# A fused state-space and channel-mix block on one core: transposed t and the gate's sums in one PSUM bank, values in another, powers interleaved, last unit in halves

## What is computed

```python
xn = layernorm(x)
A_t = sigmoid(A_param)[:, None] ** arange(L)
conv = causal_conv(xn, C_vec * A_t * B_vec) + D_vec * xn      # per channel, along the sequence
z = gelu(conv) @ W_proj.T + b_proj
y = layernorm(xn + z) * gamma + beta
t = x + layernorm(y)
ts = layernorm(t); prev = ts shifted by one row in its sequence, first row 0
r = sigmoid((mu_r * ts + (1 - mu_r) * prev) @ W_r.T)
k = square(relu((mu_k * ts + (1 - mu_k) * prev) @ W_k.T))
out = t + layernorm(r * (k @ W_v.T))
```

## Time and profile before

| | |
|---|---|
| runs | 156.83, 157.89, 156.50 us; median 156.83 |
| profiled execution | 156.51 us, of which its span (first to last instruction) 154.7 us |
| granted TensorE clock, mean | 0.986 |
| PE busy | 137.6 us (89% of the span), 955 matmuls |
| PE weight load busy | 118.0 us (76%) |
| DVE busy | 131.8 us (85%), 371 instructions |
| ACT busy | 130.9 us (85%), 391 instructions |
| POOL busy | 129.0 us (83%), 196 instructions |
| moved | 4.59 MB read, 4.19 MB written, 57 GB/s over the span |
| chain that ended last | PE 74%, DVE 9%, POOL 7%, ACT 4%, issue 2%, DMA 2% |

### The profile page before, as it was taken

How to read it: one execution, slowest core, us unless ns; L and a number is a source line. 1 busy time by engine, 2 the same in 40 slices (tenths; PEclk the granted TensorE clock), 3 DMA queues, 4 the chain that set the end, 5 groups by cost and what they waited for, 6 DMA issues and landing times.

```text
span 154.7 us, 3289 instructions
## 1 busy us (share of the span) xinstructions
PE 137.6 (89%) x955; PEld 118.0 (76%) x955; DVE 131.8 (85%) x371; ACT 130.9 (85%) x391; POOL 129.0 (83%) x196
## 2 busy tenths in 40 slices
PE   3968968887999999999999999999999999999700
PEld 3957857874979797997979977997797798777600
DVE  0999899999899899999999799899989968351783
ACT  5719999699988959988997999979988979999900
POOL 4478997998979886989999899988998989998650
PEclk9999999999999999999999999999999999999995
DMA  3789910000000000100200020020200000414444
GB/s 91 205 226 311 326 35 2 0 0 0 6 0 0 0 4 0 43 29 4 68 0 0 0 70 5 0 70 6 68 0 0 0 4 2 136 59 145 136 126 144
DMA packets 18688, 8.98 MB, mean 58 GB/s; under 512 B 1520, under 2 KB 18672, under 8 KB 18672
## 3 DMA queue, kind: packets, MB, share of 16 engines
q1 hardware_dynamic: 18384, 8.79, 19.5%
q10 hardware_dynamic: 288, 0.00, 0.1%
HBM read 4.59 MB, written 4.19 MB: 57 GB/s over the span
## 4 chain that ended last, share of the span: by engine, by line
PE 74%; DVE 9%; POOL 7%; ACT 4%; issue 2%; DMA 2%; SPq 0%; POOLq 0%; DVEq 0%
PE ps_r L669 9%; PE ps_tv L677 9%; PE ps_r L668 9%; PE ps_k L657 9%; PE ps_k L658 9%; PE ps_z L635 7%; PE ps_prefix L618 7%; PE ps_tv L648 4%; PE ps_prefix L620 3%; PE ps_z L636 3%; PE ps_xT L611 3%; POOL xn_pow L206 3%; DMA x_all<-in_x 2%; POOL x_r L193 2%; DVE x_raw L403 1%
## 5 line engine op out<-in xcount | busy, mean ns | idle before, releaser
L299 ACT ACTIVATE xn<-x_all,x_bias,x_r 128x128 f32<-128x128 f32 x64 | 26.4, 492 | 1.1 <-POOL x_bias L195 1.1
L669 PE MATMUL ps_r<-mixed_T,tsT 128*128 128x128 f32 x128 | 24.7, 275 | 0.0
L668 PE MATMUL ps_r<-mixed_T,tsT 128*128 128x128 f32 x128 | 24.7, 275 | 0.0
L356 ACT ACTIVATE f_normal<-f,out_bias,f_r 128x128 f32<-128x128 f32 x56 | 23.0, 488 | 0.4 <-POOL out_bias L249 0.4
L635 PE MATMUL ps_z<-pv_T,gelu 128*128 128x128 f32 x128 | 22.4, 277 | 0.7 <-ACT gelu L313 0.6
L206 POOL TENSOR_TENSOR xn_pow<-xn,pow_token 128x512 f32<-128x512 f32 x16 | 20.4, 1278 | 2.6 <-DVE pow_token L539 2.1
L635 PEld LDWEIGHTS ps_z<-pv_T,gelu 128*128 128x128 f32 x128 | 19.4, 191 | 1.8 <-issue 0.9
L668 PEld LDWEIGHTS ps_r<-mixed_T,tsT 128*128 128x128 f32 x128 | 19.6, 192 | 1.0 <-issue 1.0
L618 PE MATMUL ps_prefix<-prefix_ones,xn_pow 128*128 128x256 f32 x64 | 19.3, 384 | 1.0 <-POOL xn_pow L206 1.0
L669 PEld LDWEIGHTS ps_r<-mixed_T,tsT 128*128 128x128 f32 x128 | 19.4, 192 | 0.0
L319 ACT ACTIVATE junk<-ps_z 128x128 f32<-128x128 f32 x64 | 16.7, 277 | 3.1 <-PE ps_z L636 3.1
(11 more groups left out here) (86 smaller groups left out, 362.6 us busy)
## 6 DMA issues: line engine op xcount, KB each, us to landing
out_x<-x_all SPq DMA_DIRECT2D x16, 256.0 KB, 2.2
x_all<-in_x SPq DMA_DIRECT2D x7, 512.0 KB, 5.9
x_all<-in_x SPq DMA_DIRECT2D x2, 128.0 KB, 3.1
x_all<-in_x SPq DMA_DIRECT2D x1, 256.0 KB, 3.5
...
```

The lines of the kernel that those rows point to most:

```text
L299: last = a_.activation(tile(xn[u % D], j), xa(u, j), ACT.Identity, bias=col(x_bias, u, j), scale=col(x_r, u, j))
L356: last = a_.activation(tile(f_normal[u % D], j), tile(f[u % D], j), ACT.Identity, bias=col(out_bias, u, j), scale=col(f_r, u, j))
L668: t_.matmul(tile(ps_r, j), tsT[u % D][:, q, l + 1:l + 1 + P], mixed_T[:, 0, :], start=True, stop=False)
L669: last = t_.matmul(tile(ps_r, j), tsT[u % D][:, q, l:l + P], mixed_T[:, 1, :], start=False, stop=True)
```

## The change

It does the following.

- **PSUM.** Transposed t and the gate's sums share the bank ps_tr; the values have ps_v. `transpose_t(u)` now waits for `tanh_r(u - 1)` instead of `gate(u - 2)`, and `values(u)` no longer waits for a copy of transposed t. `gates(u)` waits for `copy_tT(u)` as before, which now also frees its bank.
- **Powers.** Each step waits for the one before by its own count, and unit 0's statistics and variances are placed between the steps. DVE no longer waits for the constants before them.
- **Start on PE.** 18 fillers at the start instead of 28, 18 instead of 14 after unit 0, and 10 more before transpose_xn(4); unit 0's transposes and prefix sum come before the transposes of W_proj and W_v.
- **Scales.** y's and f's statistics share one tensor, so that one product in `f_scale_of` makes both means; the product y_mean_r in `y_scale_of` is gone.
- **Last unit.** Unit 15's gate, statistics, scales, last add and store are done in two halves of two tiles.
- **T_ON_POOL** gains unit 1.
- **All four lists** are in a new order.

The diff, cut to its core (names that only follow the new tensors are left out):

```diff
-T_ON_POOL = (3, 5, 7, 9, 11, 13)
+T_ON_POOL = (1, 3, 5, 7, 9, 11, 13)
...
-        ps_xT, ps_prefix, ps_z0, ps_z1, ps_z2, ps_tv, ps_k, ps_r = (
+        ps_xT, ps_prefix, ps_z0, ps_z1, ps_z2, ps_tr, ps_k, ps_v = (
...
+            for h in range(2):
+                sp.wait_ge(out_half, h + 1)
+                sp.dma_start(out_dram[:, LAST * TILES + 2 * h:LAST * TILES + 2 * h + 2, :],
+                             xa(LAST, 2 * h, 2).rearrange("p (n c) -> p n c", c=P)).then_inc(stored, 16)
...
             def f_scale_of(u, n):
...
-                g_.tensor_tensor(cols(f_mean_r, u, n), cols(f_raw, u, n)[:, :, 1], cols(f_r, u, n),
+                g_.tensor_tensor(yf_mean_r[:, u:u + n, :, :], yf_raw[:, u:u + n, :, :, 1], yf_r[:, u:u + n, :, :],
                                  ALU.mult).then_inc(f_mean_done, n)
...
+            def f_scale_half(h):
+                j = 2 * h
+                pool.wait_ge(f_half_stats, h + 1)
+                g_.tensor_scalar(f_ve[:, LAST, j:j + 2], yf_raw[:, LAST, 1, j:j + 2, 2], 1.0 / P, 4 * EPS, ALU.mult,
+                                 ALU.add).then_inc(half_chain, 1)
...
...
-            def x_first_half(h):
+            def x_first_half_stats(h):
                 dve.wait_ge(x_first[h], 16)
-                link(pair_stats(x_raw, 2 * h, xa(0, 2 * h, 2)))
+                pair_stats(x_raw, 2 * h, xa(0, 2 * h, 2)).then_inc(x_first_stats, 1)
+            def x_first_half_variance(h):
+                dve.wait_ge(x_first_stats, h + 1)
...
+            def gate_half(h):
+                a, b = 2 * h * P, (2 * h + 2) * P
+                dve.wait_ge(tanh_done, UNITS)
+                dve.wait_ge(v_ready, UNITS)
+                after(dve, f_scaled, LAST - D + 1)
+                v_.scalar_tensor_tensor(f[LAST % D][:, a:b], tanh[LAST % D][:, a:b], 1.0, ps_v[:, a:b], ALU.add,
+                                        ALU.mult).then_inc(f_half, 1)
...
...
+            def power_step(k):
+                n = 1 << k
+                dve.wait_ge(s_powers, k + 1)
+                v_.tensor_scalar(pow_up[:, n + 1:2 * n + 1], pow_up[:, 1:n + 1], pow_up[:, n:n + 1], None,
+                                 ALU.mult).then_inc(s_powers, 1)
...
-            x_first_half(0)
-            x_first_half(1)
-            powers(0, 8).then_inc(s_powers, 1)
-            x_pooled(1, 1)
+            power_step(0)
+            x_first_half_stats(0)
+            power_step(1)
+            x_first_half_variance(0)
+            power_step(2)
+            x_first_half_stats(1)
+            power_step(3)
+            x_first_half_variance(1)
+            power_step(4)
+            power_step(5)
+            power_step(6)
+            power_step(7)
+            link(x_stats(1))
+            x_variance(1, 1).then_inc(x_moments, 1)
...
             def transpose_t(u):
...
-                after(pe, f_ready, u - 1)
+                after(pe, tanh_done, u)
...
             def values(u):
-                pe.wait_ge(tT_copied, min(u + 2, UNITS))
                 pe.wait_ge(k_act_ready, u + 1)
```

More of the change, by code:

```diff
@@ L348, in tanh_r @@
                 after(act, f_ready, u - D + 1)
-                a_.activation(tanh[u % D][:], ps_r[:], ACT.Tanh, scale=0.5).then_inc(tanh_done, 1)
+                a_.activation(tanh[u % D][:], ps_tr[:], ACT.Tanh, scale=0.5).then_inc(tanh_done, 1)
             def scale_f(u):
@@ L676, in values @@
                 for j in range(TILES):
-                    last = t_.matmul(tile(ps_tv, j), tile(k_act[u % D], j), pv_T[:, 1, :], start=True, stop=True)
+                    last = t_.matmul(tile(ps_v, j), tile(k_act[u % D], j), pv_T[:, 1, :], start=True, stop=True)
                 last.then_inc(v_ready, 1)
             centre_bias()
-            transpose_pv(); transpose_xn(0); prefix_sum(0); keep_busy(14); transpose_xn(1); prefix_sum(1)
-            project(0); prefix_sum(2); transpose_xn(2); project(1); transpose_xn(3); prefix_sum(3); project(2)
@@ L683, in _ @@
-            transpose_rk(); transpose_xn(4); prefix_sum(4); project(3); mix_weights(); prefix_sum(5)
-            transpose_xn(5); project(4); transpose_t(0); keys(0); gates(0); transpose_xn(6); transpose_t(1)
-            prefix_sum(6); project(5); values(0); keys(1); transpose_xn(7); gates(1); transpose_t(2); project(6)
-            prefix_sum(7); keys(2); values(1); prefix_sum(8); transpose_xn(8); transpose_t(3); project(7); gates(2)
-            keys(3); transpose_xn(9); prefix_sum(9); values(2); gates(3); project(8); transpose_xn(10)
@@ L688, in _ @@
-            transpose_t(4); prefix_sum(10); values(3); keys(4); project(9); gates(4); transpose_t(5); prefix_sum(11)
-            transpose_xn(11); project(10); values(4); keys(5); gates(5); transpose_t(6); prefix_sum(12)
-            transpose_xn(12); values(5); project(11); gates(6); keys(6); transpose_t(7); transpose_xn(13)
-            prefix_sum(13); project(12); keys(7); values(6); transpose_xn(14); prefix_sum(14); gates(7)
-            prefix_sum(15); transpose_t(8); project(13); values(7); keys(8); transpose_t(9); transpose_xn(15)
```

210 lines of the change are left out of this document (103 added, 107 removed).

## The result

The changed kernel takes 159.12 us (median of four runs, 159.08 to 160.39) against 156.67 for the kernel before: a ratio of 1.0164, 95% interval 1.0127 to 1.0201. The prediction was 154.0, between 152.6 and 156.6, and faster; it was wrong in sign. The profiled execution took 159.1 us, its span 157.4, 2.7 longer than before.

What follows compares the result with a forecast made beforehand. A start paced by DVE and its chain, a middle bound by PE alone, and a tail after PE's last matmul. Span 154.7 - 2.8 (lead) + 0.1 (tail) = 152.0, plus 1.8 = 153.8, given as 154.0; range 152.6 to 156.6.

Steps and rivals of the forecast that it cites:

- The lead at keys(0): Start: keys(0) at 35.45 instead of 36.48, with 1.75 us more PE work done; lead 2.8, ends 1.0 and 3.6.
- I take back 0.8: Start, DVE: 0.8 off the convolves' gain for one x_neg collision with POOL's product near 17.2; ends 0 and 1.0.
- DVE does not wait for anything in this stretch: Start: without DVE waits, convolve(0), (1) and (2) move up by 0.9, 1.2 and 1.9.
- Rival (1): Ramp swallows the gain if collisions fall twice or residual(1) slips: 155.6, no difference; chance 0.16 together with rival 2.
- PE found its inputs ready everywhere: Middle, keys(0) to values(15): by 0.05 to 0.1 at the thinnest, 0.5 or more elsewhere; cost 0.
- bound of 1.6: Middle: upper end of the cost, 16 x 0.1, if the thin places give a tenth each.
- Rival (3): Middle: shared bank opens holes, late tanh_r holds transpose_t and PE's queue; 159.4 at 0.35 per unit; chance 0.08.
- The tail: After PE's end: DVE ends 0.1 later, halved store between 0.4 earlier and later; +0.1, ends -0.3 and +0.6.
- The idle 0.44 that DVE had is filled: Tail: POOL's two chains run under DVE's adds, leaving no wait; DVE ends 0.1 later than before.
- E + 4.5: Tail: when POOL's second bias was to be ready, about 4.5 us after PE's end E.
- Rival (4): Tail: start as forecast, but POOL's queue late, +1.0: 154.8 to 155.0, still faster; chance 0.76 together with the forecast.
- rival 2: Start: fewer fillers raise PE's clock late, unit 0 takes 1.75 more: 155.6; chance 0.16 together with Rival (1).

Runs made afterwards that it cites:

- t_port: t_fix with the adds of units 13 and 14 moved behind unit 15's scale; 157.97 us, 1.0086 of the kernel before.
- m_pool1: Changed kernel with unit 1's t scaled on ACT again (T_ON_POOL without 1); 160.72 us, 1.0256 of the kernel before.
- t_whole: Changed kernel with unit 15's gate, statistics, scales, last add and store whole again; 158.42 us, 1.0125 of the kernel before.
- b_halves: Kernel before with only unit 15's gate, statistics, scales, add and store in halves; 157.51 us, 1.0050 of the kernel before.
- t_fix: Changed kernel with unit 15 whole, add_f(10) moved from POOL to DVE, add_f_late(11) behind the last statistics; 157.67 us, 1.0060 of the kernel before.
- b_adds: Kernel before with only DVE's adds of units 11 and 12 moved behind f_stats_of(15); 157.84 us, 1.0071 of the kernel before.
- t_halffix: Changed kernel, halves kept, add_f(10) moved from POOL to DVE, add_f_late(11) behind the halves' statistics; 157.71 us, 1.0060 of the kernel before.
- t_add11: Changed kernel, halves kept, add_f_late(11) moved from ahead of the gate to behind the last statistics; 158.66 us, 1.0132 of the kernel before.
- a_best: t_fix with x_stats(4) moved behind convolve(0) as well; 157.70 us, 1.0059 of the kernel before.
- b_start4: Kernel before with the change's start alone (powers, 18 fillers, unit 0 ahead of weights' transposes) and x_stats(4) behind convolve(0); 155.48 us, 0.9924 of the kernel before.

## Why the prediction was wrong

**The powers** (right). Copy of the powers forecast at 7.2, measured 7.11; first product 7.7, measured 7.62.

**The lead at keys(0)** (2.8 forecast, 1.4 found; at 36.84 instead of 35.45). The step that failed is "I take back 0.8", one collision of x_neg with POOL's product. There are two, 0.77 long at 14.68 and 1.01 at 30.97, none at 17.2, and the second falls between convolve(4) and residual(1), where the sum has x_pooled(8) at its undisturbed 0.95. convolve(3) came 0.4 late (23.88 for 23.45), convolve(4) 0.5 late (28.79 for 28.3), project(4) 1.5 late (33.23 for 31.7): that last 1.0 is the second collision (1.01 less its usual 0.17) and 0.2 more. In t_port, whose first part ran as forecast (convolve(3) at 23.24, convolve(4) at 28.15), the second collision alone is left, and keys(0) comes at 36.20, 0.75 late. "DVE does not wait for anything in this stretch" failed as well: x_stats(4) waited 1.23 for its x. That second miss cost 0.6 at most, as far as these executions show: 36.84 here, 36.20 in t_port, and the clock is in that difference too. Rival (1) named this, a collision that falls twice.

**The middle** (0 forecast, 1.7 found). The step that failed is "PE found its inputs ready everywhere". The bound of 1.6 has the right size by luck: it was to come from thin places that give a tenth each, and none of the three named, transpose_t(2), transpose_t(10) and gates(13), shows a gap over 0.1. The gaps are in six other places, where the walk had 0.5 or more to spare. The kernels with the order of before show 108.43 to 108.45 from keys(0) to values(15), those with the new order 108.36 to 108.43 with 1.75 less work (m_pool1 aside). The loop through the shared bank held as forecast, except for the copies at gates(2) and keys(15) (0.4 together); 1.1 is project waiting for residual and residual for POOL's y scale, 0.9 of it new. Rival (3) had the sign of the result, but its mechanism, a late tanh that holds transpose_t, is not in the trace.

**The tail** (+0.1 forecast, +2.3 found with the store). This step failed most, but it does not decide the sign alone: with the tail as forecast, -1.4 + 1.75 + 0.1 would still be 0.4 slower. Its parts, from the tails:

| part | forecast | found | from |
|---|---|---|---|
| halves | about 0, under the adds | +0.9 | t_whole against the changed kernel; b_halves alone 0.9 |
| add_f(10) on POOL, add 11 before the gate | not in the sum | +0.5 | t_whole 8.80, t_fix 8.27 |
| adds of 11 and 12 inside | 0.65 for add 12, filling the idle 0.44 | +1.2 | b_adds alone 1.20; t_fix less before 1.14 |
| store in halves | -0.4 to +0.4 | -0.24 | last add to end of span |

How the first two rows share their 1.4 depends on what is undone first: with POOL freed first (t_halffix) the queue is worth 1.2 and the halves 0.2.

"The idle 0.44 that DVE had is filled" is the sentence that was wrong: that wait is for POOL's last bias, and POOL's small operations slow down beside DVE's adds, so it moved along. The sum counts POOL's two chains at what they take alone, though it takes such a collision into account at the start. In b_halves, where nothing else is changed, the second bias came at E + 5.65 (151.51 less 145.86) instead of E + 4.5, and the one product of 1.39 instead of 0.19 has the size of that difference. In the changed kernel, with the queue ahead of it, it came at E + 7.35 (153.68 less 146.33). Rival (4) named the queue (add_f(10) and f_scale(14) ahead of the halves) but priced it at 1.0 and called it faster still. The Trainium skill, DMA: Bandwidth & Descriptors, section "Anatomy of one DMA — SWDGE (gpsimd) path", has a time per byte from which 0.3 follows, as an estimate, for the halved store; its figures are for DMAs that GpSimd issues. These stores are issued by SP; the traces come near it all the same (0.24 here, 0.22 in b_halves).

Why are the adds late? The new order of PE puts values two to three units behind, where before values(u) followed gates(u). The gates of units 12 and 13 start at 137.97 and 141.02, before at 132.10 and 136.94, while PE itself is 0.4 behind; ACT's scale_f(11) comes at 143.96 instead of 139.46. That b_adds has the price is shown; that the order of values is the reason for the lateness is read from the two traces and was not tried, since it needs all four lists written anew. Read from the traces and not tried, too, is that t_scale_of(2, 2) on POOL makes residual(4) late.

**The clock** (rival 2). With 18 fillers it did fall to 0.50 in the profiled executions of the changed kernel, t_add11, t_halffix and m_pool1, and not in those of the other seven. In the four, the distance of two fillers goes from 0.21 to 0.11 at 5.5 to 6.0, before the last filler; in the seven no two of the 18 are 0.11 apart, and prefix_sum(0) takes 1.3 us as in the kernel before. Where the clock fell it took 2.5. At keys(0) the four are at 36.79 to 36.84, the three others with the same start at 36.20 to 36.61, so it is worth 0.2 to 0.6 there: the mechanism is there, its size an eighth to a third of the 1.8 that the rival gave. In the changed kernel it does not reach the end (spans 157.2 and 157.4 at a mean clock of 0.962 and 0.963, 157.1 and 157.2 at 0.980 and 0.977). In a_best, where convolve(0) does not wait for x_stats(4), four executions at 0.966 to 0.968 have spans of 156.0 to 156.1, the five at 0.977 to 0.983 of 155.5 to 155.6; that this 0.5 is the start's clock was not profiled.

The account of a_best and b_start4 against before closes: -1.95 + 1.70 + 1.14 = +0.9 (span 155.5 for 154.7), and -1.27 with nothing given back (span 153.4). The start was the good part of the change, the new order of the middle and the tail the bad ones. The two leads are from one execution each, and executions with the same start differ by up to 0.6 at keys(0).
